# Turning eight normalised tiles by transposing DMAs in place of TensorE

## The reference

```
x = x + attn(layernorm(x))          # 16 heads, 1024 stored patterns each
#   attn(y) = rms_norm(softmax(q k^T) v) + y,  q = rms_norm(y) @ W_in.T @ W_q.T
h = layernorm(x)                    # rows of 2048
gate = silu((h @ w_gate) * s_gate)  # 2048 -> 8192, int8 weights
up   = (h @ w_up) * s_up
x = x + ((gate * up) @ w_down) * s_down
```

## Time and profile before

| | |
|---|---|
| Median of three runs | 1626.28 us (1625.08 to 1626.29) |
| The profiled execution, its own time | 1625.37 us |
| Its span, the slowest core, first to last instruction | 1623.7 us |
| Spans of the eight cores | 1619.0 to 1623.7 us |
| Mean granted TensorE clock | 0.998 to 0.999 |
| PE busy | 1583.5 us, 98% |
| DVE, ACT, POOL busy | 321.1, 304.3, 203.9 us |

### The profile page before, as it was taken

How to read it: one execution, slowest core, us unless ns; L and a number is a source line. 1 busy time by engine, 2 the same in 40 slices (tenths; PEclk the granted TensorE clock), 3 DMA queues, 4 the chain that set the end, 5 groups by cost and what they waited for, 6 DMA issues and landing times.

```text
span 1623.7 us, 20461 instructions; the slowest of 8 cores (1619.0 to 1623.7 us)
## 1 busy us (share of the span) xinstructions
PE 1583.5 (98%) x8232; PEld 763.4 (47%) x8395; DVE 321.1 (20%) x610; ACT 304.3 (19%) x388; POOL 203.9 (13%) x424
## 2 busy tenths in 40 slices
PE   4999999999999999999999999999999999999998
PEld 3555556444444444444444444444444444444443
DVE  4355465382110000000000000000000200201102
ACT  5677657221110000000000000000000100100200
POOL 4232243111110000000000000000010000000000
PEclk9999999999999999999999999999999999999999
DMA  8974665465442222222222222221252522523411
GB/s 179 175 144 93 143 170 157 157 232 198 145 151 78 78 78 78 78 78 78 78 78 78 78 78 75 70 73 70 90 181 78 182 78 78 177 72 99 159 52 53
DMA packets 52083, 181.44 MB, mean 112 GB/s; under 512 B 5904, under 2 KB 6416, under 8 KB 48656
## 3 DMA queue, kind: packets, MB, share of 16 engines
q0 software_dynamic: 38592, 135.94, 28.3%
q1 hardware_dynamic: 8640, 35.72, 6.1%
q10 hardware_dynamic: 4752, 8.40, 1.9%
HBM read 126.17 MB, written 16.78 MB: 88 GB/s over the span
## 4 chain that ended last, share of the span: by engine, by line
PE 96%; DMA 2%; issue 1%; DVE 0%; POOL 0%; ACT 0%; SPq 0%; DVEq 0%; POOLq 0%; ACTq 0%
PE PS L892 54%; PE PS L1032 27%; PE PS L549 6%; PE PS L630 3%; PE PS L586 3%; DMA arena<-winT 1%; DMA arena<-x 1%; PE PS L351 1%; PE PS L518 0%; PE PS L511 0%; POOL arena L342 0%; PE PS L570 0%; POOL arena L94 0%; ACT arena L592 0%; DVE arena L366 0%
## 5 line engine op out<-in xcount | busy, mean ns | idle before, releaser
L892 PE MATMUL PS<-arena 128*128 128x512 bf16 x4013 | 880.4, 379 | 4.4
L892 PEld LDWEIGHTS PS<-arena 128*128 128x128 bf16 x4096 | 400.4, 98 | 481.6
L1032 PE MATMUL PS<-arena 128*128 128x512 bf16 x2007 | 440.0, 379 | 2.2
L1032 PEld LDWEIGHTS PS<-arena 128*128 128x128 bf16 x2048 | 200.4, 98 | 241.6
L912 DVE SCALAR_TENSOR_TENSOR arena<-PS,cols_s,arena 128x1024 bf16<-128x1024 f32 (+1 forms) x78 | 85.1, 1092 | 741.8 <-PE PS L892 730.1
L909 ACT ACTIVATE arena<-PS,cols_s 128x1024 bf16<-128x1024 f32 (+1 forms) x78 | 75.0, 961 | 784.4 <-PE PS L892 764.8
L94 POOL DMA_DIRECT2D arena<-wg x78 | 41.4, 531 | 793.1 <-PE PS L892 723.5
L592 ACT ACTIVATE arena<-PS 128x1024 bf16<-128x1024 f32 x128 | 128.0, 1022 | 48.2 <-PE PS L586 47.9
L549 PE MATMUL PS<-arena 128*128 128x512 bf16 x490 | 117.4, 380 | 2.5 <-DMA arena<-winT 2.0
L1018 DVE TENSOR_TENSOR arena<-PS,arena 128x512 f32<-128x512 f32 (+1 forms) x33 | 22.3, 674 | 392.3 <-PE PS L1032 392.3
L1009 ACT ACTIVATE arena<-arena,c_s 128x512 f32<-128x512 f32 x32 | 25.5, 811 | 322.9 <-DVE arena L1021 308.0
(11 more groups left out here) (89 smaller groups left out, 386.8 us busy)
## 6 DMA issues: line engine op xcount, KB each, us to landing
arena<-wg POOLq DMA_DIRECT2D x78, 512.0 KB, 3.5
arena<-wu POOLq DMA_DIRECT2D x78, 512.0 KB, 4.3
arena<-wd POOLq DMA_DIRECT2D x64, 512.0 KB, 3.6
arena<-x SPq DMA_DIRECT2D x16, 1024.0 KB, 7.4
arena<-winT POOLq DMA_DIRECT2D x31, 512.0 KB, 7.1
x1sp<-arena SPq DMA_DIRECT2D x8, 1024.0 KB, 4.7
arena<-x1sp ACTq DMA_DIRECT2D x32, 256.0 KB, 6.1
out<-arena SPq DMA_DIRECT2D x31, 256.0 KB, 5.1
```

Source lines behind the costliest of these rows:

```text
L892: f = lambda En, n=n, hf=hf, hc=hc, b0=b0, w=w: En.matmul(bank(b0 + n), w[:, hc * 128:(hc + 1) * 128], x1T[hf][:, hc, :], start=(hc == 0), ...
L1032: return lambda En: En.matmul(bank(j), fuse[:, ic, j * 128:(j + 1) * 128], wdb[(q * 16 + g) % 8][:, c * 512:(c + 1) * 512], start=(ic == 0 ...
```

## The change

The eight transposes and the copy of each part go. A new method of a DMA slot issues one transposing DMA for a whole tile of 128 x 2048 bf16 (512 KB) from `ns[j % 2]` into `x1T[hf]`, on the queue of SP, at the position of `x1n` and behind it (and behind the load of x that `x1n` issues). It waits for `x1n`, and `nsfree[j % 2]` is now the DMA's completion. Gate and up wait for the DMAs. Two semaphores take turns. The turning of the rows for the attention, with the same helper `transposed`, stays on TensorE.

```diff
+    def turned(self, lane, dst, src, *toks):
+        lane.wait(*toks)
+        self.n += 16
+        lane.ops.append(lambda En, d=dst, s=src, h=self.sem: En.dma_start_transpose(out=d, in_=s).then_inc(h, 16))
+        return (self.sem, self.n)
...
+        s_xt = [Slot(sem("dxt%d" % i)) for i in range(2)]
...
-            def x1T_part(hf, j, k0, b):
-                pb, t = transposed(b, ns[j % 2], k0, 8, t_x1n[j])
-                if k0 == 8:
-                    nsfree[j % 2] = t
+
+            def x1T_tile(hf, j):
                 o = (j % 4) * 128
-                t = dve.tick(lambda En: En.tensor_copy(x1T[hf][:, k0:k0 + 8, o:o + 128], pb), t)
-                bank_free[b] = [t]
+                t = s_xt[j % 2].turned(sp, x1T[hf][:, :, o:o + 128], ns[j % 2], t_x1n[j])
+                nsfree[j % 2] = t
                 t_x1T[hf].append(t)
...
-                def x1T_of(j, pos):
-                    for k, k0 in enumerate((0, 8)):
-                        at(pos[k], lambda k0=k0: x1T_part(hf, j, k0, banks[(k0 // 8) % len(banks)]))
...
-                        x1T_of(j, (p1 + 2, p1 + 4))
+                        at(p1, lambda j=j: x1T_tile(hf, j))
...
-                        x1T_of(j, (p0 + 10, p0 + 12))
+                        at(p0 + 8, lambda j=j: x1T_tile(hf, j))
```

More of the change, by code:

```diff
@@ L663, in layer, with rows_g @@
             t_ssq = {}
-            def x1T_part(hf, j, k0, b):
-                pb, t = transposed(b, ns[j % 2], k0, 8, t_x1n[j])
-                if k0 == 8:
-                    nsfree[j % 2] = t
+            def x1T_tile(hf, j):
                 o = (j % 4) * 128
-                t = dve.tick(lambda En: En.tensor_copy(x1T[hf][:, k0:k0 + 8, o:o + 128], pb), t)
-                bank_free[b] = [t]
+                t = s_xt[j % 2].turned(sp, x1T[hf][:, :, o:o + 128], ns[j % 2], t_x1n[j])
+                nsfree[j % 2] = t
                 t_x1T[hf].append(t)
-            def rows_g(hf, banks, eng):
+            def rows_g(hf, eng):
                 j0 = hf * 4
@@ L811, in slow_attention @@
                 for hf, eng in ((0, pool), (1, dve)):
-                    for _, f in rows_g(hf, [7], eng):
+                    for _, f in rows_g(hf, eng):
                         f()
@@ L831, in layer @@
                     if s == H + 1:
-                        side = rows_g(0, [7], pool)
+                        side = rows_g(0, pool)
                     nxt = None
@@ L848, in layer @@
                 assert not side
-                side = rows_g(1, [6, 7], dve)
+                side = rows_g(1, dve)
             fuse = bv(O_FUSE, IC * T).rearrange("p (ic t) -> p ic t", t=T)
@@ L1068, in _build_nc @@
         outs_fast = layer(False)
-        slots_all = [s_cols, s_sc, s_mats, s_wr, s_sd] + s_x + s_w + s_pat + s_spill + s_wd + s_xg + s_xr + s_out
+        slots_all = [s_cols, s_sc, s_mats, s_wr, s_sd] + s_x + s_w + s_pat + s_spill + s_wd + s_xg + s_xt + s_xr + s_out
         ends = [(e.sem, e.n) for e in (pe, act, dve, pool, sp) if e.n] + [(e.sem, e.n) for e in slots_all]
```

## The result

The changed kernel took 1655.11 us in the median of four runs, against 1625.77 us of the kernel before on the same chip: 1.0172 times as long, with an interval of 1.0158 to 1.0187. It is 28 us slower by the ratio, where 3.4 us faster was forecast, and 15 us above the range.

A forecast was written before the change was run, and what follows sets the result against it. TensorE was taken as the bound: 6.1 us of transposes removed, less 1.7 us of waiting at item 0 and 1.0 of clock, gave -3.4 us, so 1622.9 us. The range was 1619.0 to 1640 us.

The forecast's parts named there:

- What bounds the kernel: Whole kernel: TensorE, busy 98% of the span; removing its instructions wins time, and nothing else matters unless TensorE waits.
- One group of transposes 0.44 us: On TensorE, a group of eight transposes costs 0.44 us, so 0.89 us a tile.
- second half 3.6: Beside gate and up, removing the transposes of four tiles at 0.89 us each wins 3.6 us, all of it.
- First half 2.5: Up to item 0, removing eight groups wins 2.5 us; tile 1's and tile 2's first groups win nothing.
- the longer idle stretch costs no clock: At tile 1, TensorE's longer idle stretch could cost up to 1.7 us of clock; taken as nothing.
- at half the plain rate: Transposing DMAs run at half the plain rate; tile 3's lands 1.7 us late for item 0, behind the load of x.
- What queues behind the DMAs otherwise: Spills, ACT's squares of tile 6, item 14 and weights behind or beside the DMAs all have time to spare; no cost.
- Clock: Item 0's wait makes TensorE run at a lower granted clock: 1.0 us, between nothing and 1.7.
- slow transposes: Rival, 27%: DMAs land so late that item 0 waits over 4.4 us and the gain is used up.
- case of 21 us behind the load: Under slow DMAs: item 0 waits 17.7 us, item 14 8, clock 3.4; net +23, 1649 us; squares' wait unpriced.
- Weights late: Rival, 8%: second-half DMAs make weight pairs late, four waits of 1 to 3 us: -2 to +6, 1624 to 1632.

The follow-up runs named there:

- experiment 2: Changed kernel with transposing DMAs only for tiles 4 to 7, tiles 0 to 3 turned on TensorE as in the kernel before: 1624.55 us, 0.9999.
- experiment 8: Changed kernel, but tile 3 on TensorE, the other seven tiles' DMAs ahead of their load of x, squares' junk written elsewhere: 1629.28 us, 1.0031.
- 11: Kernel before, with 24 more long-satisfied waits in SP's program and no transposing DMA: 1626.5 us in one execution.
- experiment 4: Changed kernel with the transposing DMA issued ahead of the load of x on SP's queue, not behind it: 1632.85 us, 1.0041.
- experiment 3: Changed kernel with plain copies in 256-byte pieces, blocks not turned, in place of the transposing DMAs: 1630.68 us, 1.0038.
- experiment 7: Changed kernel without the last six loads of W_in on POOL's queue: 1633.81 us, 1.0051.
- experiment 1: Changed kernel with the squares' junk written to an unused corner of x1T, not the buffer the DMA reads: 1643.01 us, 1.0091.
- experiments 8 to 10: Seven tiles by DMA, tile 3 on TensorE: 1629.28 us; then load of x first again from tile 4 on: 1627.24; then 96 more SP waits: 1626.55.
- 10: Seven tiles by DMA, tile 3 on TensorE, load of x first from tile 4 on, plus 96 long-satisfied waits on SP: 1626.55 us, 1.0006.
- 5: Changed kernel with plain copies in 4-KB rows, data neither turned nor placed by block, in place of transposing DMAs: 1626.22 us, 1.0009.

## Why the prediction was wrong

**What bounds the kernel: right.** TensorE waits, or else the time is its work. That is why its waits, some 32 us on core 2, came through to the end.

**One group of transposes 0.44 us, second half 3.6: right.** 3.5 measured (experiment 2).

**First half 2.5: of the right size, not seen in full.** The successor of L351, L358, ran 128 times, none after 200 us, as forecast. Tile 1's wait is in one piece, 2.54 us to 232.51, as said; tile 2's grew to some 1.0 to 1.3 us. Without tile 3, 1.8 were forecast and 1.5 found (experiment 8). That the longer idle stretch costs no clock was optimistic: with the short stretch (the kernel before, experiments 2 and 11) 7 cores of 24 ran products near it at the lower level, with the long one (all others) 50 of 80, at 1.7 us each.

**Added, "at half the plain rate": the step that failed.** From it came 9.6 us to landing for tile 3. It was 14.7 to 20.0, and item 0 waited 6.6 to 11.9 us instead of 1.7. Of the two terms behind that number, the load of x ahead took 5.8 to 7.9 us, not 4.9, and the DMA landed 7.2 to 13.5 us after the load, not 5.0. The rate isn't the fault: with no load ahead of it such a DMA lands in 4.2 us at the least and 6.2 to 7.4 in the median of a core (experiment 4), which is half the rate of the plain 3.5 us, as taken. The fault was to make it one number and to add it to the load's. Small pieces behind 1 MB and beside four weight loads land in 9.1 to 14.0 us even when plain (experiment 3), and turned in 13.7 to 18.5 (experiment 7). I shared out the bandwidth by bytes, 210 GB/s to each, as if the engines would still move 420 in all. They moved 104 beside tile 1's DMA (240 to 260 us), and 250 while tile 3's was in flight on core 2 (last number):

```profile
295.60:310.30 14.70, 7.67 (x74) 5.06 (x74) 2.98 (x9) 7.08 (x8) 2.19 (x4) 0.84 0.85 250
```

The two pages of the Trainium skill that I weighed: Advanced Engine Details and Errata (X-Bar Transpose), as fast as plain DMAs, holds here only in good company: 4.2 us at the least against 3.5 of a plain load, and 5.9 to 7.5 against 6.0 to 6.9 of a plain copy in the places of tiles 6 and 7. Behind a load of x and beside loads on POOL's queue tile 1's took 10.6 to 29.3 us, and up to 32.5 in experiment 1, and there it doesn't hold. VectorE: DVE Perf Modes (The three transpose paths), 1309 ns for a block, doesn't add up over the sixteen blocks of a DMA, which would be an estimated 21 us; alone it took 4.2.

**"What queues behind the DMAs otherwise": the second step that failed, and the dearer.** I looked at the squares of tile 6 behind tile 2's DMA, issued with an idle queue around it; it took 8.7 to 11.2 us and held. I didn't look at the squares of tile 5 behind tile 1's, where a load of W_in runs beside it: 237.19 to position 36 at 244.3 is 7 us of cover on core 2, and it took 29.3. Even the 7 us were less than the order of the code gives: `x1n` ended at 231.5, but the load of x between them waited for a late spill, a path that I didn't have at all. The statement "the engines are mostly idle there" was made of one place and not of all four. Taking the buffer away gave 13 us (experiment 1), taking the loads of W_in away 20 (experiment 7).

**Clock: the mechanism was right, the size small.** I priced 1.0 us at item 0. On core 2 gate and up took 894.1 us, and should have taken 889.6 - 3.5, and 3.3 for the wait for wg: 4.7 us are left. The granted clock accounts for 4.5 of them: it was at the lower level for 5.6 us right behind item 0's wait, which loses 2.8, and for 3.4 us behind the wait for wg at 373.9, which loses 1.7. Behind item 0's wait it was 1.7 to 2.9 us on the eight cores.

**Rivals.** It was slow transposes, and its case of 21 us behind the load, with the squares' wait named and not priced, came to 1649; measured 1655. That the two lie near each other is chance: item 0 waited 6.6 to 11.9 us and not 17.7, and the squares, which have no price there, made up for it. Its wait at item 14 didn't come, since the DMAs of tiles 5 to 7 landed in 5.9 to 11.1 us. Weights late was real as well, 3.3 us on core 2.

**Not foreseen: the end, +1.9 us.** It takes over half of the 3.5 us of the second half and is why experiment 2 is no faster.

**Still open.** What inside the DMA engines stretches the packets when both queues are active: the runs show the condition (experiments 4 and 7) and the price per packet, not the mechanism. Also why weights are late on some cores and not on others in experiments 8 to 10. No version here beats the kernel before. Experiments 2 and 10 come level; so does 5, but it doesn't turn the tiles.

## What to carry to other kernels

Before you hand work to a DMA, list every instruction that next touches its source, its destination and its queue, each with its own cover; the one you leave out is the one that decides. Take the time of a new kind of DMA from its worst company, with bulk loads on both queues, and not from bytes over bandwidth: 512 KB were 4.2 us in good company and 32 in bad. And when a change gains 3 us on each core, look at the slowest of the eight and at the end of the program before you count it.

## What the hardware showed that I hadn't expected

- A transposing DMA of 512 KB keeps SP's sequencer busy 1.3 us when the queue is idle and 5 to 13 us behind another DMA; a plain copy of as many 256-byte pieces 0.6 us, of 4-KB rows 0.47.
- DMA engines at a share of 1.16 moved 104 GB/s, with 82% of the packets under 512 bytes (1404 of 1721), against 420 at 1.13. Small packets alone aren't slow: in experiment 7, 94% of them were that small, and each took a third of the time.
- Where a transposing DMA is slow, its neighbours are too: on core 2 the spill of 1 MB behind tile 1's took 22.6 us and the load of W_in beside it 21.6, where the same two took 4.0 and 5.9 before. Without loads of W_in the spills behind it are quick, 4.1 us (experiment 7).
- 24 satisfied waits in SP's program, near its start, made the end of the kernel, far later, about 2 us longer (one execution, all eight cores).
